# Issue order of two loads per tile in a mixture-of-experts stage: the rows of tile g+1 ahead of the weights of tile g

## The reference

```
h = concat(tokenizer(x), txt)                       # 32 x 192 x 128
h = h + attention_block(layernorm(h))               # 8 heads
xf = layernorm(h) as 6144 rows of 128
idx, gates = top-2 of xf @ router_w, softmax        # 8 experts
for e in range(8):
    y = layernorm(xf + relu(xf @ w1[e] + b1[e]) @ w2[e] + b2[e]) * gamma[e] + beta[e]
    out += (gate of e, where e was chosen) * y
h = h + out
```

## Time and profile before

| | us |
|---|---|
| median of 3 runs | 572.75 |
| lowest and highest | 570.62, 575.18 |
| profiled execution, its own time | 568.6 |
| its span, first to last instruction | 566.8 |

### The profile page before, as it was taken

The page is one execution under the profiler, slowest core; times in us unless marked ns, Lnnn a source line. Parts: engine busy times, 40 slices in busy tenths (PEclk is TensorE's granted clock), DMA queues, the critical chain, the costliest instruction groups (busy, mean ns, idle before and its releaser), DMA issues. The chain is left out here.

```text
span 566.8 us, 15143 instructions
## 1 busy us (share of the span) xinstructions
PE 460.1 (81%) x4392; PEld 360.0 (64%) x4392; DVE 444.3 (78%) x1768; ACT 343.5 (61%) x793; POOL 307.7 (54%) x447
## 2 busy tenths in 40 slices
PE   3676787888897888889889789899899999999800
PEld 3454444555564565446555479799798999999800
DVE  5865756897865788886887859689987888888897
ACT  4464555776764776667657554764555556666562
POOL 2541022348785267575686667876676555455430
PEclk9777987998997899889889899899999999999955
DMA  5156637455367232132421476677899889999598
GB/s 167 46 154 192 152 118 166 104 120 123 94 176 179 63 114 73 55 104 74 114 73 33 133 256 191 192 229 251 266 301 302 268 291 310 302 306 304 186 337 248
DMA packets 75075, 101.56 MB, mean 179 GB/s; under 512 B 10750, under 2 KB 58785, under 8 KB 74994
## 3 DMA queue, kind: packets, MB, share of 16 engines
q1 hardware_dynamic: 54114, 77.61, 47.1%
q0 software_dynamic: 6416, 12.93, 6.5%
q10 hardware_dynamic: 14464, 10.06, 6.0%
HBM read 74.40 MB, written 32.38 MB: 188 GB/s over the span
## 5 line engine op out<-in xcount | busy, mean ns | idle before, releaser
L1642 POOL DMA_INDIRECT expert_d<-pexs,dest x103 | 103.0, 1000 | 71.3 <-DVE pexs L1430 42.4
L1131 DVE TENSOR_REDUCE mx<-mbk 128x4 f32<-128x768 f32 x96 | 91.2, 950 | 40.2 <-PE mbk L814 39.7
L1628 POOL DMA_INDIRECT sorted_d<-pay,slot x96 | 96.7, 1008 | 36.1 <-issue 25.4
L630 ACT ACTIVATE pexs<-sbk 128x768 f32<-128x768 f32 x96 | 77.5, 807 | 26.4 <-PE sbk L841 24.8
L671 ACT ACTIVATE pexs<-sbk,stk 128x256 f32<-128x256 f32 (+1 forms) x152 | 58.9, 455 | 17.6 <-PE sbk L939 16.8
L939 PE MATMUL sbk<-pexs,stk 128*128 128x256 f32 (+1 forms) x304 | 68.4, 369 | 0.7 <-ACT pexs L671 0.3
L939 PEld LDWEIGHTS sbk<-pexs,stk 128*128 128x128 f32 x304 | 52.7, 193 | 6.4 <-issue 1.3
L814 PE MATMUL mbk<-stk 48*64 48x192 f16 (+1 forms) x512 | 35.5, 267 | 21.0 <-DVE mx L1131 13.5
L841 PE MATMUL sbk<-stk 49*64 49x192 f16 (+1 forms) x512 | 36.0, 266 | 16.4 <-ACT pexs L630 10.5
L1591 POOL TENSOR_TENSOR kept<-h,lnb 128x384 f32<-128x384 f32 x16 | 16.0, 1000 | 53.9 <-DVE h L1106 53.8
L814 PEld LDWEIGHTS mbk<-stk 48*64 48x64 f16 (+1 forms) x512 | 13.8, 104 | 43.0 <-issue 34.9
(11 more groups left out here) (250 smaller groups left out, 1111.7 us busy)
## 6 DMA issues: line engine op xcount, KB each, us to landing
stk<-pack_d SPq DMA_DIRECT2D x38, 706.5 KB
pexs<-pack_d SPq DMA_DIRECT2D x18, 706.5 KB, 5.8
stack_d<-kq ACTq DMA_DIRECT2D x48, 192.0 KB, 3.1
stk<-stack_d SPq DMA_DIRECT2D x64, 144.0 KB, 3.0
xn<-sorted_d SPq DMA_DIRECT2D x47, 132.0 KB
pack_d<-in_w SPq DMA_DIRECT2D x16, 256.0 KB
xin<-in_xp SPq DMA_DIRECT2D x16, 128.0 KB, 4.9
h<-in_txt SPq DMA_DIRECT2D x16, 128.0 KB, 3.2
```

Source lines behind the costliest of these rows:

```text
L630: act.activation(pex[p % 2][m][:, :, :], sbk[:, :, 0:COLS], ACT.Exp, scale=0.25).then_inc(a_pex, 1)
L1131: dve.tensor_reduce(dst, mbk[:, :, 0:COLS].rearrange("p h (c s) -> p h c s", c=2), AX.X, ALU.max).then_inc(d_mx, 1)
L1628: pool.indirect_dma_start(sorted_d[:, :], bass.IndirectOffsetOnAxis(ap=slot[p % 6][:, 2 * k + w:2 * k + w + 1], axis=0), pay[p % 6][:, k, ...
L1642: pool.indirect_dma_start(expert_d[:, :], bass.IndirectOffsetOnAxis(ap=dest[fin % 6][:, k:k + 1], axis=0), ye[fin % 4][:, k, :], None, bou ...
```

## The change

From tile 6 on, SP issues the rows one tile further ahead: load(6), load(7), load_weights(6), load(8), load_weights(7), and so on. The waits that stood ahead of load(28) stay with it, and so come ahead of load_weights(27). load(56) does not exist and is left out. Buffers, sizes, waits of each load and all other engines are as before.

```diff
-            for g in range(6, GRID):
+            def load_rows(g):
                 if g == EARLY:
                     sp.wait_ge(plan_made, 3)
                     for p in range(PAIRS - 6, PAIRS):
                         after_dma(sp, sent, p, 6)
                     sp.wait_ge(pads_sent, 16)
                     sp.wait_ge(tails_sent, 16 * NE)
-                load(g)
+                if g < GRID:
+                    load(g)
+
+            load_rows(6)
+            for g in range(6, GRID):
+                load_rows(g + 1)
                 load_weights(g)
                 if 0 <= g - PAD_AT < NE:
                     pad(g - PAD_AT)
```

## The result

| | before | after |
|---|---|---|
| median of 14 runs, us | 568.65 | 568.84 |
| lowest and highest, us | 559.02, 575.18 | 567.61, 572.72 |
| profiled execution, us | 568.6 | 569.19 |

The ratio after / before is given as 1.0087, interval 1.0057 to 1.0117; it is taken over a part of the executions (those near each kernel's fastest), and the medians over all of them stand as 1.0003. The means over all 14 are 569.22 and 569.43 us, a ratio of 1.0004; without the one execution of 559.02 us the mean before is 570.00, above that of after. So the comparison says slower by 0.9%, within the 1% that I had called no change, and on the other side of my forecast of 0.9 us faster; but that 0.9% is in the shortest executions of the kernel before, and not in all of them.

The account below looks back on a forecast made before the run. The prediction took PE to bound the expert stage, with 3.0 us of gaps on rows to win; a 2.1 us wait for weights at tile 23 left 0.9. From the median, 572.75, that gave 571.8 us, range 567.5 to 575.5.

Parts of the forecast that it names:

- What bounds: Expert stage: PE bounds, with no break except 3.01 us of gaps on rows between 400 and 430 us; clock 1.00.
- The value of the rows one tile earlier: Gaps ahead of turning rows at tiles 18, 19 and 24 all go: up to 3.0 us won.
- Weights 0.7 us later: SP's queue: each load of weights leaves one slot later, behind a load of rows, 0.7 us later than before.
- Waits for weights in place of those for rows: Tiles 19 to 23: about 2 us of new PE waits, 2.1 at tile 23, leaving a gain of 0.9 us.
- Nothing is added: All engines: the change adds no instruction on any of them.
- The waits ahead of load(28), cost 0: SP: these waits now hold load_weights(27) too, but the scatters and pads are issued before; cost 0.
- Slower in the mixed tiles: Rival, tiles 36 to 53: weights become late in mixed full and half tiles, giving 575.5 to 580 us; chance 0.08.
- The total: Whole kernel: the gain of 0.9 us taken from the median of 572.75 us gives 571.8 us.
- The range: Whole kernel: 569.7 less 2.2 to 573.4 plus 2.1, so 567.5 to 575.5 us.

Follow-up runs that it names:

- e10: The kernel before, unedited, measured against itself a second time: ratio 0.9982 (0.9939 to 1.0024), median 568.62 us, stage 168.92 us.
- e2: The changed kernel, unedited, measured again against the kernel before: ratio 1.0023 (0.9982 to 1.0064), median 570.46 us, stage 165.96 us.
- e9: The changed kernel, unedited, measured a third time against the kernel before: ratio 1.0021 (0.9978 to 1.0065), median 569.67 us, stage 165.11 us.
- e7: The changed kernel with the eight pads issued by ScalarE behind tiles 16 to 23: ratio to the kernel before 1.0025 (0.9967 to 1.0083), stage 166.64 us.
- e6: The kernel before with the new order of loads from tile 28 on only: ratio 1.0043 (0.9986 to 1.01), stage 165.73 us.
- e5: The change doubled, rows of tile g+2 ahead of weights of tile g: ratio to the kernel before 1.0334 (1.0253 to 1.0416), stage 184.53 us.
- e1: The kernel before, unedited, measured against itself: ratio 1.0019 (0.998 to 1.0057), median 570.28 us, stage 165.40 us.
- e12: The changed kernel with pads issued by ScalarE and weights 27 ahead of the waits for load(28): ratio to the kernel before 1.0046 (0.9998 to 1.0093), stage 165.85 us.
- e8: The kernel before with the rows of tiles 12 to 27 issued by ScalarE, three tiles ahead: ratio 1.0145 (1.0079 to 1.0212), stage 173.60 us.

## Why the prediction was right or wrong

**What bounds.** Right: PE is full but for waits on loads, with its clock at 1.00 in both profiles. Too certain: "PE alone to the end of the stage", for e10 has a gap of 0.74 us at 471.91, and "nothing is lost to the clock there", for e10 lost 1.7 us to it.

**The value of the rows one tile earlier.** The mechanism was right: no gap on rows in after, e2 or e9. The size, "up to 3.0 us", came from one execution; others of the same kernel have 0.93 and 3.11.

**Weights 0.7 us later.** Right: 0.81 us behind `ye` in place of 0.22, so 0.6.

**Waits for weights in place of those for rows.** Right in kind, smaller in size: 2 us "together, at tiles 19 to 23" were 1.16 us at tiles 18, 20 and 25, in e2 1.49, in e9 0.75. The one wait from which the net gain was worked out, 2.1 us at tile 23 from a landing of 8.0 us, didn't come in any of the three profiles; in after weights 23, issued at 420.83, had landed by 428.17, in 7.3 us or less. So up to tile 23 the gain was 428.56 - (428.17 - 1.40) = 1.8 us, twice the forecast, and 0.6 of it was lost at tile 25. That the stage gained 0.98 us, with 0.9 forecast, is luck in part. Over three profiles each the means differ by 1.4 us, without e10 by 0.5, and of the pairs with the pads elsewhere none is shorter in the new order (165.31 and 165.35; 165.50 against 166.64 and 165.85): a gain of about a microsecond fits the runs and is not shown by them.

**Nothing is added.** The issue of rows 25 took 2.08 us (SP's timeline above) and held weights 24 and 25; the last gap of 0.40 us stands on it. I had no such term.

**The waits ahead of load(28), cost 0.** Right in the changed kernel. e7 shows their price when the scatters and the pads end later: 1.17 us.

**Slower in the mixed tiles.** It didn't happen (e6); weights 53, for which the margin was put at 0.3 us, were late once, by 0.21 us in e2. The price was not overdone: e5, with weights held for another step, lost 17 us where I expected 12 or more.

**The total.** This step failed: "The same 0.9 us from the median, 572.75, is 571.8". It carried a gain of the stage over to the median of three runs, and so put what the rest of the execution does by itself at nothing, with no row for it. The median of 14 runs of the same kernel is 568.65, 4.1 us lower, and the point was 3.0 us above the result. What the runs showed in its place: the part ahead of the changed loads differs by more than the gain. It was 1.40 us longer in the profiled pair, all of it before the turn of tile 1, while the stage won 0.98; in the three profiles of before it spreads by 4.9 us, and e1 and e9, one of each kernel, differ by 0.3. The first comparison came out at 1.0087, against the sign of the forecast, and the repeats at 1.0023 and 1.0021 with the kernel before at 1.0019 and 0.9982. No profile shows a cost of the change that could make 0.9%: the front part shifts before the order differs, the stage is not longer, and behind the last up the three profiles of after take 35.1 to 35.8 us, those of before 35.5 to 35.6. The numbers of the first comparison put it on the short executions of the kernel before, above all the one at 559.02 us (the next is 565.64). Why these were short, and why the changed kernel had none such in that batch, stays open; an effect of some tenths of a per cent in the whole time does too.

**The range.** It reads 2.1 and 2.4 us off the three runs and adds 2.2 and 2.1; with the numbers as read it is 567.6 to 575.8.

## What to carry to other kernels

When two loads of one in-order queue are swapped so that the first to be needed leaves first, the other one inherits its wait: look up the slack of the one that is put back before counting the gaps of the one that is put forward. A gap that the profile shows is one draw; profile the unchanged kernel two or three times before taking its size as the value of removing it. And where a stage gains a microsecond in an execution that spreads by ten, measure the stage between two fixed instructions, not the total, look at a third one ahead of the first changed instruction to see what was shifted before it, and let the unchanged kernel run against itself beside it.

## What the runs showed of the hardware

**Granted clock and time.** In the 35 runs of the kernel before beside e9 to e12, the six with the highest mean clock (0.923 to 0.927) took 562.68 to 566.64 us and the six with the lowest (0.898 to 0.902) 570.09 to 576.43. That goes together; that the clock is the cause is not shown. The clock differs in the front part; in the expert stage it is 1.00 in both first profiles, and falls behind the longest gaps: 0.81 from 414 to 420 us in e10 (gap of 2.08 us), 0.77 in e5 (2.77), 0.50 in e8 (4.84). The first 200 us of the profile before, then of the profile after (columns as in the earlier trace rows):

```profile
0.00:100.00 100.00, 68.12 (x513) 45.20 (x513) 65.99 (x185) 53.15 (x98) 27.96 (x87) 0.83 0.52 142
100.00:200.00 100.00, 83.64 (x1049) 55.39 (x1050) 74.94 (x287) 67.60 (x138) 56.38 (x90) 0.93 0.50 121
```

```profile
0.00:100.00 100.00, 69.72 (x561) 44.91 (x561) 67.38 (x187) 55.00 (x103) 27.94 (x87) 0.90 0.52 144
100.00:200.00 100.00, 84.23 (x1002) 55.72 (x999) 73.63 (x282) 65.87 (x133) 56.62 (x90) 0.89 0.48 119
```

**Issues that take long.** In the expert stage a DMA issue on SP or ScalarE took 0.34 to 0.44 us as a rule and now and then 0.6 to 0.9, but 1.36 us once in e7 (SP), 2.08 in after (SP) and 3.85 in e8 (ScalarE), and what stood behind the last two on their engine came later by as much. In the front part there are such issues in several profiles, up to 2.35 us (ScalarE, e9, at 62.35). What holds them no view shows.
